# Turning the next input and the keys on VectorE in 32 by 32 blocks, instead of on TensorE, in a fused mLSTM and MLP block

## The reference

```python
x = L0_attn_x
xn = _layernorm(x, axis=-1)
x = x + _L0_attn_ref(xn, Wq, Wk, Wv, Wog, Wig, big, Wfg, bfg, gamma, Wout) \
      + _L0_ffn_ref(xn, w_gate, w_up, w_down)
# mLSTM, 8 heads, per token t of a sequence:
m_new = max(f_log + m, i_t);  F = exp(f_log + m - m_new);  I = exp(i_t - m_new)
C = F * C + (I * k_t) outer v_t;   n = F * n + I * k_t
h = (q_t * scale) @ C / (max(|q_t*scale . n|, exp(-m_new)) + EPS)
y = (sigmoid(o) * multihead_norm(h)) @ Wout.T
# FFN, hidden size 2048:
out = (silu(xn @ w_gate.T) * (xn @ w_up.T)) @ w_down.T
```

## Time and profile before

| | |
|---|---|
| median of 3 runs | 3138.32 us (3137.84 to 3140.11) |
| the profiled execution | 3138.3 us, its span 3136.5 us |
| PE busy | 3084.2 us, 98% of the span |
| DVE busy | 1907.1 us, 61% |
| ACT busy | 1126.0 us, 36% |
| POOL busy | 751.1 us, 24% |
| granted PE clock, mean | 0.998 of full |
| DMA | 51.09 MB, mean 16 GB/s |

### The profile page before, as it was taken

One profiled execution on the slowest core, in us unless ns is written; L12 is line 12 of the kernel. 1 busy time (PEld: TensorE's weight loads), 2 busy tenths in 40 slices (PEclk: granted clock), 3 DMA queues, 4 the chain that ended last, 5 costly groups with the idle time before them and its releaser, 6 DMA issues.

```text
span 3136.5 us, 61859 instructions
## 1 busy us (share of the span) xinstructions
PE 3084.2 (98%) x22474; PEld 2240.3 (71%) x22474; DVE 1907.1 (61%) x4377; ACT 1126.0 (36%) x2160; POOL 751.1 (24%) x1120
## 2 busy tenths in 40 slices
PE   4999999999999999999999999999999999999999
PEld 2677777777777777777777777777777777777776
DVE  8666656656556656555666566565566665565665
ACT  6333333333333333333333333333233333333332
POOL 4222222222222222222222222212222212222222
PEclk9999999999999999999999999999999999999999
DMA  5000000000000000000000000000000000000000
GB/s 222 8 14 13 13 7 7 13 13 13 13 6 8 13 13 13 7 7 13 13 13 13 7 7 13 13 13 13 0 13 13 13 13 7 7 13 13 13 13 7
DMA packets 20334, 51.09 MB, mean 16 GB/s; under 512 B 1506, under 2 KB 1634, under 8 KB 18274
## 3 DMA queue, kind: packets, MB, share of 16 engines
q1 hardware_dynamic: 20322, 50.95, 4.4%
HBM read 34.16 MB, written 16.78 MB: 16 GB/s over the span
## 4 chain that ended last, share of the span: by engine, by line
PE 97%; DVE 1%; ACT 1%; issue 0%; DMA 0%; SPq 0%; DVEq 0%; ACTq 0%
PE work L1082 21%; PE work L1084 21%; PE work L1083 21%; PE acc L1083 7%; PE acc L1084 7%; PE acc L1082 7%; PE o_bank L1195 3%; PE o_bank L1255 2%; PE work L1261 2%; PE s_bank L1242 1%; PE work L1273 1%; PE work L1267 1%; PE e_bank L1236 1%; PE work L1172 1%; PE work L1227 1%; DVE amax L740 1%
## 5 line engine op out<-in xcount | busy, mean ns | idle before, releaser
L1082 PE MATMUL work<-xt,weights 128*128 128x256 f16 x4608 | 1256.0, 273 | 0.5 <-DVE arena L958 0.5
L1084 PE MATMUL work<-xt,weights 128*128 128x256 f16 x4608 | 1256.0, 273 | 0.0
L1083 PE MATMUL work<-xt,weights 128*128 128x256 f16 x4608 | 1255.9, 273 | 0.0
L543 POOL TENSOR_TENSOR arena<-arena 128x256 f16<-128x256 f32 x512 | 348.4, 680 | 1715.7 <-ACT arena L678 1715.7
L955 DVE SCALAR_TENSOR_TENSOR arena<-arena,work 128x256 f32<-128x256 f32 x512 | 215.2, 420 | 538.1 <-ACT arena L674 534.9
L1082 PEld LDWEIGHTS work<-xt,weights 128*128 128x128 f16 x4608 | 478.5, 104 | 69.9 <-DVE arena L958 0.7
L1083 PEld LDWEIGHTS work<-xt,weights 128*128 128x128 f16 x4608 | 450.9, 98 | 69.5
L1084 PEld LDWEIGHTS work<-xt,weights 128*128 128x128 f16 x4608 | 450.8, 98 | 52.2
L674 ACT ACTIVATE arena<-work,unscale 128x256 f32<-128x256 f32 x512 | 241.7, 472 | 585.6 <-PE work L1084 585.2
L678 ACT ACTIVATE arena<-arena 128x256 f16<-128x256 f32 x512 | 213.3, 417 | 592.2 <-DVE arena L958 592.2
L1082 PE MATMUL acc<-weights,arena 128*128 128x512 f16 x1024 | 388.1, 379 | 0.4 <-POOL arena L543 0.4
(11 more groups left out here) (214 smaller groups left out, 4038.1 us busy)
## 6 DMA issues: line engine op xcount, KB each, us to landing
arena<-x_dram SPq DMA_DIRECT2D x33, 512.0 KB, 3.3
out_dram<-arena SPq DMA_DIRECT2D x32, 512.0 KB, 2.8
weights<-w_g_dram SPq DMA_DIRECT2D x4, 1024.0 KB, 12.6
weights<-w_u_dram SPq DMA_DIRECT2D x4, 1024.0 KB, 20.4
arena<-w_d_dram SPq DMA_DIRECT2D x4, 1024.0 KB, 26.8
arena<-w_qk_dram SPq DMA_DIRECT2D x1, 1024.0 KB, 5.8
arena<-w_v_dram SPq DMA_DIRECT2D x1, 1024.0 KB, 7.8
weights<-w_o_dram SPq DMA_DIRECT2D x1, 1024.0 KB, 25.3
```

The costliest lines, as they stand in the source:

```text
L543: g.tensor_tensor(hh[:, j % HB, 1, :], tt[:, j % 2, :], hh[:, j % HB, 0, :], ALU.subtract).then_inc(h_ready, 1)
L1082: t.matmul(dst, w[0], a[0], start=first, stop=False, skip_group_check=True)
L1083: t.matmul(dst, w[0], a[1], start=False, stop=False, skip_group_check=True)
L1084: return t.matmul(dst, w[1], a[0], start=False, stop=last, skip_group_check=True)
```

## The change

The banks lose three uses (`kT`, `xT0`, `xT1`), and PE loses their 12 transposes per block. VectorE does the turning instead, with transposes of 32 by 32 blocks: one instruction takes 32 partitions and four such blocks (128 float32 per partition) to another set of 32 partitions.

- `turn(dst, src, q)` turns 32 tokens of a chunk with four instructions, one for each quarter of the features' partitions. A chunk needs q = 0 to 3, a block 8 turns, 32 instructions. They stand in the steps `turn00` to `turn13` (chunk, quarter).
- `kturn0` to `kturn3` turn the keys, four instructions each (one for each head of a group), 16 in a block. `kT` on DVE now reads SBUF instead of a bank.
- `mean_var` moves from after ffn5 to after ffn3, `xn0` from 6 to 4, `xn1` from 9 to 6, `kT` from 4 to 5. ACT's `xn0` additionally waits for `qi_ready`, `xn1` for `kt_ready`: they write over `qs` and `kf`. The turned input lies in `kp` and over `lf` and `ip`.
- ACT's and DVE's `xT` steps split the turned input from SBUF; ACT starts them once `hoT1` is in its bank. PE waits for `xt_ready` ahead of each block's gates.
- On DVE alone, after ffn10, `pv2` (drain of the third state product) stands ahead of `es3`.
- Ahead of the loop, the first block's normalised input lies in `kk`, and POOL clears `qq`, `kk` and others after the first turn of it.

```diff
-USES = ([..., "ffn4", "wbc", "kT", "ffn5", ..., "ffn15", "hoT1", "xT0", "xT1", "att1"])
+USES = ([..., "ffn4", "wbc", "ffn5", ..., "ffn15", "hoT1", "att1"])
...
-AFTER[3] = ["wT", "stack3"]
-AFTER[4] = ["wbc", "kT", "es0"]
-AFTER[5] = ["o0", "mean_var"]
-AFTER[6] = ["es1", "pv0", "xn0"]
+AFTER[3] = ["wT", "stack3", "mean_var"]
+AFTER[4] = ["wbc", "es0", "kturn0", "kturn1", "xn0"]
+AFTER[5] = ["o0", "kturn2", "kturn3", "kT", "turn00"]
+AFTER[6] = ["es1", "pv0", "turn01", "xn1"]
+AFTER[7] = ["turn02", "turn03", "turn10"]
 AFTER[8] = ["es2", "pv1", "center0"]
-AFTER[9] = ["scale0", "xn1"]
+AFTER[9] = ["scale0", "turn11"]
 AFTER[10] = ["heads0", "es3", "pv2"]
-AFTER[11] = ["hoT0"]
+AFTER[11] = ["hoT0", "turn12", "turn13"]
...
+DVE_AFTER = {j: list(steps) for j, steps in AFTER.items()}
+DVE_AFTER[10] = ["heads0", "pv2", "es3"]
...
+            def turn(dst, src, q):
+
+                tokens = slice(q * 32, (q + 1) * 32)
+                for r in range(P // 32):
+                    features = src[tokens, :].rearrange("t (k r f) -> t r k f", k=KC, f=32)[:, r, :, :]
+                    d.transpose(dst.rearrange("p (k t) -> p k t", k=KC)[r * 32:(r + 1) * 32, :, tokens],
+                                features).then_inc(xn_turned, 1)
...
                         elif step == "kT":
 
-                            wait_full(dve, i, "kT")
+                            own.settle(dve, i)
...
+                        elif step.startswith("turn"):
+                            c = int(step[-2])
+                            dve.wait_ge(xn_ready, NCH * (i + 1) + c + 1)
+                            turn(xnt[c], xn[c], k_)
+                        elif step.startswith("kturn"):
+
+                            tokens = slice(k_ * 32, (k_ + 1) * 32)
+                            for h in range(HG):
+                                own.step(d.transpose(
+                                    k_turned.rearrange("p c g h e -> p g c h e")[tokens, :, :, h, :],
+                                    kf.rearrange("p g (c t) -> p g c t", c=NCH)[h * DQ:(h + 1) * DQ, :, :, tokens]))
...
-                pe.wait_ge(work_free[bank_no("xT1")], START + i * uses_of(bank_no("xT1")))
+                pe.wait_ge(xt_ready, NCH * (i + 1))
...
-                            wait_drained(pe, i, "kT")
+                            pe.wait_ge(kt_ready, i + 1)
```

More of the change, by code:

```diff
@@ L52 @@
 LN_EPS, EPS = 1e-5, 1e-6
-USES = (["gates", "q", "k", "v0", "v1", "ffn0", "ffn1", "ffn2", "ffn3", "wT", "ffn4", "wbc", "kT", "ffn5", "o0",
+USES = (["gates", "q", "k", "v0", "v1", "ffn0", "ffn1", "ffn2", "ffn3", "wT", "ffn4", "wbc", "ffn5", "o0",
          "ffn6", "st0", "ffn7", "ffn8", "st1", "ffn9", "ffn10", "st2", "ffn11", "hoT0", "ffn12", "st3", "o1",
-         "ffn13", "att0", "ffn14", "ffn15", "hoT1", "xT0", "xT1", "att1"])
+         "ffn13", "att0", "ffn14", "ffn15", "hoT1", "att1"])
 NUSE = len(USES)
-assert NUSE % 3 == 0
+BANK = {name: n % 3 for n, name in enumerate(USES)}
 def bank_no(name):
-    return USES.index(name) % 3
+    return BANK[name]
 def uses_of(b, before=NUSE):
-    return len(USES[b:before:3])
+    return len([name for name in USES[:before] if BANK[name] == b])
 AFTER = {j: [] for j in range(NJ)}
@@ L139 @@
 START = 1
-DVE_OWN = 58
+DVE_OWN = 74
 class Count:
@@ L239, in mlstm_mlp_kernel @@
             at[name] = arena[:, starts[name]:starts[name] + n]
-        assert 5 * SLOT + GCOLS <= starts["xn"]
+        assert 5 * SLOT + GCOLS <= starts["qq"]
         def in_arena(n):
@@ L256, in mlstm_mlp_kernel @@
         xin = at["xin"].rearrange("p (c d) -> p c d", c=NCH)
-        xn = at["xn"].rearrange("p (c d) -> p c d", c=NCH)
+        xn_first = at["kk"].rearrange("p (c d) -> p c d", c=NCH)
+        xn = at["qs"], at["kf"]
+        xnt = at["kp"], arena[:, starts["lf"]:starts["lf"] + D]
+        k_turned = arena[:, starts["bc"]:starts["bc"] + D].rearrange("p (c g h e) -> p c g h e", c=NCH, g=NG, h=HG)
         qs = at["qs"].rearrange("p (g t) -> p g t", g=NG)
@@ L331, in mlstm_mlp_kernel @@
         xt_hi = sem("xt_hi")
+        xn_turned = sem("xn_turned")
+        kt_ready = sem("kt_ready")
         xt_ready = sem("xt_ready")
@@ L514, in _ @@
             link(g.memset(uhl, 0.0))
+            pool.wait_ge(first_xt, NCH)
             for name in ("qq", "kk", "wr", "tg", "state"):
@@ L604, in x_high, with norm_x @@
                              ACT.Copy).then_inc(xt_hi, 1)
-            def norm_x(i, c):
-                act.wait_ge(factors_ready, i + 1)
-                s.activation(xn[:, c, :], xin[:, c, :], ACT.Identity, bias=shift[:, c:c + 1],
+            def norm_x(dst, c):
+                s.activation(dst, xin[:, c, :], ACT.Identity, bias=shift[:, c:c + 1],
                              scale=rstd[:, c:c + 1]).then_inc(xn_ready, 1)
+            act.wait_ge(factors_ready, 1)
             for c in range(NCH):
-                norm_x(0, c)
+                norm_x(xn_first[:, c, :], c)
                 act.wait_ge(first_xt, c + 1)
@@ L710, in _ @@
                         elif step.startswith("xn"):
-                            norm_x(i + 1, k)
+                            if k == 0:
+                                act.wait_ge(factors_ready, i + 2)
+                                act.wait_ge(qi_ready, i + 1)
+                            else:
+                                act.wait_ge(kt_ready, i + 1)
+                            norm_x(xn[k], k)
                         elif step.startswith("xT"):
-                            wait_full(act, i, step)
-                            x_high(i + 1, k, bank(step)[:, :])
+                            wait_full(act, i, "hoT1")
+                            act.wait_ge(xn_turned, START + (i * NCH + k + 1) * TURNS)
+                            x_high(i + 1, k, xnt[k])
                 own.close()
@@ L800, in means, with x_low @@
                     d.bn_aggr(mean_var[:, c, :], bn6[:, c, :]).then_inc(stats_ready, 1)
-            def x_low(i, c, src, done):
+            def turn(dst, src, q):
[4 more added lines that the diff above has]
+                                features).then_inc(xn_turned, 1)
+            def x_low(i, c, src):
                 dve.wait_ge(xt_hi, NCH * i + c + 1)
                 d.tensor_tensor(xt[:, :, 1, c * P:(c + 1) * P], src.rearrange("p (k t) -> p k t", k=KC),
-                                xt[:, :, 0, c * P:(c + 1) * P], ALU.subtract).then_inc(done, 1)
+                                xt[:, :, 0, c * P:(c + 1) * P], ALU.subtract).then_inc(xt_ready, 1)
             back = 1.0 / (XS * WS)
@@ L825, in _ @@
             for c in range(NCH):
-                x_low(0, c, (e_bank, s_bank)[c][:, :], xt_ready)
+                x_low(0, c, (e_bank, s_bank)[c][:, :])
             scales(0)
@@ L960, in _ @@
                                            op1=ALU.mult).then_inc(free_of(f"ffn{j}"), 1)
-                    for step in AFTER[j]:
+                    for step in DVE_AFTER[j]:
                         k_ = int(step[-1]) if step[-1].isdigit() else 0
@@ L986, in _ @@
                         elif step == "kT":
-                            wait_full(dve, i, "kT")
+                            own.settle(dve, i)
                             wait_drained(dve, i, "wT")
                             d.tensor_tensor(kt[:, :, :].rearrange("p c (h e) -> p c h e", h=NH),
-                                            bank("kT")[:, :].rearrange("p (c h e) -> p c h e", c=NCH, h=NH),
+                                            k_turned.rearrange("p c g h e -> p c (g h) e"),
                                             wtok[:, :, 32:32 + NH].unsqueeze(3).broadcast_to((P, NCH, NH, DQ)),
-                                            ALU.mult).then_inc(free_of("kT"), 1)
+                                            ALU.mult).then_inc(kt_ready, 1)
                         elif step.startswith("es"):
@@ L1061, in _ @@
                         elif step.startswith("xT"):
-                            wait_full(dve, i, step)
-                            x_low(i + 1, k_, bank(step)[:, :], free_of(step))
+                            x_low(i + 1, k_, xnt[k_])
+                        elif step.startswith("turn"):
[8 more added lines that the diff above has]
+                                    kf.rearrange("p g (c t) -> p g c t", c=NCH)[h * DQ:(h + 1) * DQ, :, :, tokens]))
                         elif step == "att0":
@@ L1105, in _ @@
                 for k in range(KC):
-                    tr = t.transpose((e_bank, s_bank)[c][:, k * P:(k + 1) * P], xn[:, c, k * P:(k + 1) * P],
+                    tr = t.transpose((e_bank, s_bank)[c][:, k * P:(k + 1) * P], xn_first[:, c, k * P:(k + 1) * P],
                                      ident[:, :])
@@ L1221, in _ @@
                             mm_.then_inc(work_full, 1)
[L1222 to L1229, removed]
                         elif step.startswith("es"):
@@ L1263, in _ @@
                                      stop=True).then_inc(work_full, 1)
[L1264 to L1269, removed]
```

6 lines of the change are left out of this document (3 added, 3 removed).

## The result

| | before | after |
|---|---|---|
| median | 3139.22 us (4 runs, 3137.84 to 3140.45) | 3110.1 us (4 runs, 3109.16 to 3110.74) |
| profiled execution, its span | 3138.3, 3136.5 us | 3110.6, 3108.9 us |
| PE, DVE busy | 98%, 61% | 98%, 75% |

The ratio is 0.9908, 95% interval 0.9896 to 0.9919: 29.1 us faster, 0.91 us in each of 32 blocks, where 1.36 had been removed from PE. The first rival came true, not the forecast's time.

What follows compares the result with a forecast made beforehand. PE, 98% busy and never waiting in the loop, bounds the kernel; removing 1.36 us in each of 32 blocks gives 3138.3 - 43.5 = 3094.8, with zero stall. Forecast 3095 us (3091 to 3101, chance 0.48), range 3089 to 3134.

Steps and rivals of the forecast that it cites:

- The first rival: At hoT0, heads0 late by part of the gain: 3098 to 3120 us for T = 0.33; chance 0.22.
- just in time: stall zero: At hoT0, hof ready between 1669.8 and 1670.5, wanted at 1670.43: room -0.07 to +0.7 us, read as no stall.
- PE's saving: Key turn 0.49 and input turn 0.87 us leave PE, by starts: 1.36 us a block, 43.5 us in all.
- The rival that took durations: On PE, turns save durations, not starts: 1.70 x 32 = 54.4 us, down to 3084 us; chance 0.05.
- The price of a transpose: On DVE, T = 0.31 us start to start, taken from copies of 32 partitions; bounds 0.20 and 0.44.
- the prediction's walk: DVE's chain timed from es0 (1636.8) to heads0 (begins 1667.8), with hof ready between 1669.8 and 1670.5.
- All on the path: On DVE ahead of heads0, all 40 transposes lengthen the path, since each tanh is done when DVE comes.
- the second rival: Same wait at hoT0, price above the gain: slower or no gain, 3238 to 3260 us at T = 0.44; chance 0.18.
- The third edit: On DVE after ffn10, st2's drain (pv2) ahead of es3: worth 0 to 19 us beside the turns, nothing by itself.
- The keys: kT on DVE done at 1644.1, PE wants kt at 1645.6: 1.5 us of room.
- The gates: PE's gates after its xt_ready wait come behind the input's split, which ends with hoT1's: no cost.
- The cover at the block's end: POOL's low part of ffn15 before down(15): 0.18 us of room stays; rival of up to 0.1 us a block, chance 0.07.

Runs made afterwards that it cites:

- Four kernels without the wait: Changed kernel with turn10 moved to step 13, 3094.9 us; turns in DVE's waits, 3095.53; that with es3 before pv2, 3095.36; input transposes paired, 3094.82.
- the run with es3 first: Changed kernel with es3's product put back ahead of pv2, the third state drain, on DVE: 3151.68 us, ratio 1.0040.
- the first experiment: Changed kernel with turn11's four transposes moved from behind scale0 to step 13, ahead of att0: 3120.48 us, ratio 0.9943.
- the kernel with the turns in waits: Changed kernel with kturn0, turn01 and turn11 placed ahead of es0, es1 and es2 on DVE, where it waits for POOL's mask: 3095.53 us, ratio 0.9862.
- the one with paired transposes: Changed kernel with input transposes of chunks 0 and 1 paired by same quarters, only eight of them ahead of heads0: 3094.82 us, ratio 0.9859.

## Why the prediction had the saving and the tight place right, and the time 15 us low

The forecast was "just in time: stall zero" at hoT0, and that step failed: PE waits there in every block. The place, the path to it and the wait stood in the prediction as its first rival, whose 3098 to 3120 us for T = 0.33 holds the measured 3110.1; the forecast's own 3091 to 3101 does not.

- **PE's saving** was right. Four kernels without the wait stand at 3094.8 to 3095.5 us against 3138.6 to 3139.4, 43 to 45 us; 43.5 was forecast, from starts. The rival that took durations (54 us) falls.
- **The price of a transpose** was mis-sized, 0.31 for 0.333 us, and this term made the miss. 40 x 0.023 = 0.9 us. DVE's chain shows it growing: es0 begins 31.94 us after the gates (1623.71 - 1591.77), exactly as in the prediction's walk (1636.8 - 1604.86), and heads0, 40 transposes later, begins at 63.88 (1655.65 - 1591.77) against 62.94 (1667.8 - 1604.86). The walk put the end of heads0 at 64.9 to 65.6 us after the gates (1669.8 to 1670.5, less 1604.86); with 0.9 more, 65.8 to 66.5; it was 65.84. The term was taken from copies of the same partitions because they also change quarters. The gap of 0.03 us behind the end is the same here, but a transpose is 302 ns long where those copies are 270 to 280, and no row of before could show that. On a path of 40, where 0.01 us becomes 0.4 us a block, the first rival should have had at least the weight of the forecast.
- **The signal's way** was left out at the very place where the room was nearly nil: 0.15 us from L1078's end to PE's start. (It is not the same everywhere: in the run with es3 first, PE starts ffn12 0.06 us after the drain's end at 1680.86.) Both terms together: 65.84 + 0.15 against 65.58 is 0.41 us; the 0.03 by which hoT0 itself got longer makes 0.44; 3095.7 + 32 x 0.44 = 3109.8 us. Measured 3110.1.
- **"All on the path"** was wrong for turn11, which lies beside POOL's power. The total was right because heads0 then took 1.96 us (1655.65 to 1657.61), the lower of the prediction's two bounds; that turn11 lay in a shadow would have misled whoever picked turn11 to move, and it misled me in the first experiment. Nor is the chain without idle time, as the second rival had it: DVE waits 2.03 us for a mask ahead of es1 and again ahead of es2. The mask comes out of DVE's own drains, by way of ACT and POOL, so such a wait moves along with the chain and makes up for nothing late; only work that is put into it is free.
- **The third edit** was priced at 0 to 19 us beside the turns. It is worth 42: the sum had es3's 0.67 us and not its wait for the mask, 0.74 us. Alone it is worth nothing, as said.
- **The keys** came in time: ready at 1631.40, wanted at 1632.51, 1.1 us of room where 1.5 was forecast.
- **The gates** come 2.39 us behind the input's split, which ends at 1682.59 + 1.28 = 1683.87, with the gates at 1686.26. The prediction said "more than 3", where its own numbers give 2.8. Nothing waits there.
- **The cover at the block's end** held, as narrow as forecast. In the kernel with the turns in waits, low part of ffn15 and down(15):
```profile
1673.45 0.67 POOL L559 TENSOR_TENSOR arena<-arena 128x256 f16<-128x256 f32 x1 [3.11 <-ACT arena L693]
```
```profile
1674.29 0.38 PE L1121 MATMUL acc<-weights,arena 128*128 128x512 f16 x1
```
1674.12 to 1674.29 is 0.17 us; 0.18 was forecast, and PE starts 0.22 us behind the matmul before, as in the rest of the row.

The version to keep is any of the four with all 48 transposes on DVE and no wait. Of them the one with paired transposes also leaves DVE least to do: 616.09 us in the window of 820, against 633.80 with the turns in the waits. Their times do not differ beyond their intervals.

## What to carry to other kernels

When work moves from a full engine to one that is 61% busy, what counts is not its idle share but the one place where the full engine waits for it: count the moved instructions ahead of that place, and multiply every uncertainty of their price by that count. Then place them by what the receiving engine waits for anyway (a mask, a power on POOL), since four such instructions cost -10 us in the shadow of POOL's power, 43 as a second four behind them, and nothing in step 13. Order on an in-order engine is free until the room is gone, and then costs the whole wait of whatever stands in front.

## What was not expected of the hardware

- Some of DVE's instructions and POOL's disturb each other both ways. Beside L1078 (0.95 us instead of 0.69), POOL's one-element L562 took 0.63 us instead of 0.18 and the low part before it 0.81 instead of 0.67:
```profile
1653.57 1.64 POOL L574 TENSOR_TENSOR small<-small,half_pow 128x8 f32<-128x8 f32 x1 [0.51 <-DVE small L1068]
1656.26 0.81 POOL L555 TENSOR_TENSOR arena<-arena 128x256 f16<-128x256 f32 x1 [1.05 <-ACT arena L689]
1657.03 0.63 POOL L562 TENSOR_TENSOR begun<-half_pow 1x1 f32<-1x1 f32 x1
```
- The transposes are not among them. They kept to 0.30 us beside POOL's power, and in this and the other kernels also beside its low parts and masks (the slowest 0.31), and POOL's low part kept to its 0.67 beside them. It is not that they have one input only: a copy has one too, and in the kernel before the next copy behind those of the earlier trace rows took 0.75 us instead of 0.28 beside POOL's low part. What makes the difference no run here shows. The prediction's doubt, that DVE's transposes might slow POOL, is answered by it.
```profile
1621.40 0.75 DVE L908 COPY arena<-arena 32x512 f16<-32x512 f16 x1
```
```profile
1621.30 0.71 POOL L543 TENSOR_TENSOR arena<-arena 128x256 f16<-128x256 f32 x1 [3.22 <-ACT arena L678]
```
- A float32 transpose of 128x128 costs PE 0.109 us in a row of them (0.87 / 8), while the same block on DVE takes four instructions and 1.33 us, or 1.05 in pairs (two pairs, 1656.19 to 1657.24). The exchange pays only because PE is full and DVE is not.
